# The order of five queues: all attention products ahead of the first FFN group's matmuls

## What is computed

```python
csum = jnp.cumsum(jax.nn.log_sigmoid(ftilde), axis=-1)       # ftilde, itilde: linear gates of [q,k,v]
Dtilde = where(tril, csum_i - csum_j, -inf) + itilde_j
max_d = jnp.max(Dtilde, axis=-1, keepdims=True)
Ctilde = jnp.einsum('bhid,bhjd->bhij', qh, kh) * jnp.exp(Dtilde - max_d) / TAU
maxit = jnp.maximum(jnp.abs(jnp.sum(Ctilde, -1, keepdims=True)), jnp.exp(-max_d))
Htilde = jnp.einsum('bhij,bhjd->bhid', Ctilde, vh) / (maxit + 1e-06)
x = x + groupnorm_per_head(Htilde) * gn_w + gn_b
xf = layernorm(x)
h = jax.nn.silu(jnp.einsum('nd,edf->nef', xf, w1))
routed = jnp.einsum('ne,ned->nd', combine, jnp.einsum('nef,efd->ned', h, w2))
shared = jax.nn.sigmoid(xf @ shared_gate_w) * ((jax.nn.silu(gate) * up) @ shared_down)
out = x + routed + shared
```

## Time and profile before

| | |
|---|---|
| median of 3 runs | 161.49 us (159.48 to 164.11) |
| the profiled execution's own time | 158.38 us |
| its span in the profile | 156.3 us |
| TensorE matmul busy | 132.2 us, 85% |
| VectorE busy | 133.6 us, 85% |
| ScalarE busy | 78.8 us, 50% |
| GpSimd busy | 66.4 us, 43% |
| granted TensorE clock, mean | 0.967 |

### The profile page before, as it was taken

How to read it: one execution, slowest core, us unless ns; L and a number is a source line. 1 busy time by engine, 2 the same in 40 slices (tenths; PEclk the granted TensorE clock), 3 DMA queues, 4 the chain that set the end, 5 groups by cost and what they waited for, 6 DMA issues and landing times.

```text
span 156.3 us, 4033 instructions
## 1 busy us (share of the span) xinstructions
PE 132.2 (85%) x1347; PEld 94.2 (60%) x1347; DVE 133.6 (85%) x511; ACT 78.8 (50%) x159; POOL 66.4 (43%) x134
## 2 busy tenths in 40 slices
PE   0566286499998978999989999988999999999990
PEld 0446175055764846536754688755677878788870
DVE  5999996947789899799999799999997989959882
ACT  3179967383124234553475635595567858251210
POOL 8765860898767899491554331026020000000000
PEclk9999999999968998579999999999999999999999
DMA  5998221471120001100000000000200011002002
GB/s 152 292 274 215 52 42 37 114 213 20 20 52 13 6 8 40 29 6 0 0 4 0 6 0 0 4 0 0 73 0 2 0 34 38 2 0 67 4 0 67
DMA packets 13268, 7.38 MB, mean 47 GB/s; under 512 B 1680, under 2 KB 12960, under 8 KB 13248
## 3 DMA queue, kind: packets, MB, share of 16 engines
q1 hardware_dynamic: 13072, 6.96, 17.7%
q10 hardware_dynamic: 176, 0.17, 0.5%
HBM read 4.83 MB, written 1.05 MB: 38 GB/s over the span
## 4 chain that ended last, share of the span: by engine, by line
PE 47%; DVE 35%; issue 7%; SPq 5%; DMA 1%; ACT 1%; POOL 1%; DVEq 1%; POOLq 0%
PE bank L984 16%; PE bank L966 12%; DVE xs L1441 7%; PE bank L888 5%; PE bank L929 5%; PE bank L900 4%; SPq L264 3%; PE bank L872 3%; DVE ct L1285 2%; DVE qblk L1447 2%; DVE st L1178 2%; DVE vsum L1213 2%; DVE newt L1356 1%; DVE vs L1343 1%; DMA mr<-pm 1%
## 5 line engine op out<-in xcount | busy, mean ns | idle before, releaser
L1441 DVE SCALAR_TENSOR_TENSOR xs<-bank,comb,xs 128x128 f32<-128x128 f32 x128 | 35.9, 344 | 4.9 <-PE bank L984 4.2
L984 PEld LDWEIGHTS bank<-w,hh 128*128 128x128 f32 x288 | 36.3, 191 | 5.6 <-issue 1.1
L984 PE MATMUL bank<-w,hh 128*128 128x128 f32 x288 | 37.9, 277 | 0.7 <-DVE xs L1441 0.3
L647 ACT ACTIVATE hh<-bank 128x512 f32<-128x512 f32 x36 | 21.3, 597 | 25.6 <-PE bank L966 25.2
L966 PE MATMUL bank<-xnT,w 128*128 128x512 f16 x120 | 31.1, 382 | 0.8 <-DVE hh L1430 0.8
L929 PEld LDWEIGHTS bank<-vx,ct 64*64 64x64 f32 x512 | 16.0, 135 | 3.9 <-issue 3.4
L966 PEld LDWEIGHTS bank<-xnT,w 128*128 128x128 f16 x120 | 11.4, 99 | 9.9 <-issue 2.7
L929 PE MATMUL bank<-vx,ct 64*64 64x17 f32 x512 | 17.2, 208 | 0.1
L403 POOL TENSOR_TENSOR kw<-vx,tok 128x128 f32<-128x128 f32 x32 | 12.9, 432 | 8.2 <-DVE tok L1275 4.2
L888 PE MATMUL bank<-qblk,kT 128*64 128x512 f16 x96 | 15.1, 420 | 1.2 <-DVE ct L1285 1.2
L600 ACT ACTIVATE dd<-bank 128x512 f32<-128x512 f32 x16 | 9.2, 592 | 13.1 <-PE bank L872 12.6
(11 more groups left out here) (129 smaller groups left out, 231.2 us busy)
## 6 DMA issues: line engine op xcount, KB each, us to landing
xs<-in_x SPq DMA_DIRECT2D x4, 256.0 KB, 4.8
cx<-in_ctx SPq DMA_DIRECT2D x4, 256.0 KB, 5.2
qblk<-qT SPq DMA_DIRECT2D x32, 32.0 KB, 2.0
w<-in_w SPq DMA_DIRECT2D x2, 512.0 KB, 4.4
out<-xs SPq DMA_DIRECT2D x4, 256.0 KB, 2.5
mr<-in_mr SPq DMA_DIRECT2D x2, 384.0 KB, 6.7
gl<-in_gl SPq DMA_DIRECT2D x1, 384.0 KB, 5.1
mr<-pm SPq DMA_DIRECT2D x12, 8.0 KB, 1.9
```

The lines of the kernel that those rows point to most:

```text
L647: A.activation(hh[:, e], pH[e % 2][:, :], ACT.Silu).then_inc(silu_ready, 1)
L984: ins = pe.matmul(pO[n % 2][:, t * P:(t + 1) * P], hh[:, e, t * P:(t + 1) * P], w2[:, e], start=True, stop=True)
L1441: ins = V.scalar_tensor_tensor(ob[:, a], pO[n % 2][:, t * P:(t + 1) * P], comb[:, f % 2, t, e:e + 1], (ob if e else x2)[:, a], ALU.mult, A ...
```

## The change

Only the order of calls in the lists of TensorE, VectorE, ScalarE and GpSimd changes. No instruction is added, except that ScalarE's list has four table loads fewer (six instead of ten); the list of transfers is untouched. On TensorE the five FFN calls named above go behind `intra(7, 1)`, and the order of `hidden` and `down` behind that point is another. On ScalarE all silus of group 0 stand behind `router_exp(1)`. On VectorE the accumulates of group 0 stand behind `token_stats(6)`, and `gate_up(f)` stands earlier. Some calls of the attention stage are swapped with a neighbour. The new order on TensorE (the old one is on the lines with a minus):

```diff
@@ tensor: swaps ahead of batch 4
             turn_q(1)
+            turn_ctx(3)
             turn_gates(0)
-            turn_ctx(3)
...
             intra(0, 1)
+            inter(1)
             pairs(2, 0)
-            inter(1)
...
             scores(2, 0)
+            pairs(2, 1)
             states(2)
-            pairs(2, 1)
@@ tensor: from batch 4 on
             scores(4, 0)
-            hidden(0, 0)
             inter(5)
-            hidden(0, 1)
             scores(4, 1)
             intra(4, 0)
             scores(5, 0)
             intra(4, 1)
             scores(5, 1)
-            down(0, 0)
+            intra(5, 0)
             states(6)
-            intra(5, 0)
             pairs(6, 0)
             intra(5, 1)
+            scores(6, 0)
             inter(6)
-            scores(6, 0)
             pairs(6, 1)
+            pairs(7, 0)
             xn_turn(1)
+            pairs(7, 1)
+            scores(6, 1)
             states(7)
-            pairs(7, 0)
-            pairs(7, 1)
-            hidden(0, 2)
-            scores(6, 1)
             intra(6, 0)
+            scores(7, 0)
             inter(7)
-            scores(7, 0)
             intra(6, 1)
             scores(7, 1)
+            intra(7, 0)
             logits(1)
+            intra(7, 1)
+            hidden(0, 0)
+            hidden(0, 1)
+            xn_turn(2)
+            hidden(0, 2)
+            hidden(0, 3)
+            down(0, 0)
+            hidden(0, 4)
+            hidden(0, 5)
             down(0, 1)
-            intra(7, 0)
-            intra(7, 1)
-            hidden(0, 3)
...
@@ scalar
             router_exp(0)
-            silu_table()
-            silu(0, 0)
-            silu(0, 1)
             normalise_again(2)
             square(4)
-            exp_table()
             head_log(4)
...
+            head_log(6)
+            head_exp(6)
+            square(7)
+            router_exp(1)
+            silu_table()
+            silu(0, 0)
+            silu(0, 1)
+            silu(0, 2)
...
@@ vector
             masked_states(6)
-            accumulate(0, 0)
             sums(5)
             refine_root(4)
+            weigh_scores(6, 0)
             between(6)
-            weigh_scores(6, 0)
...
+            between(7)
             weigh_scores(7, 1)
+            denominator(6)
             take_logits(1)
-            between(7)
+            variance(6)
+            sums(7)
+            route_top(1)
+            denominator(7)
+            route_chosen(1)
+            refine_root(6)
+            route_weights(1)
+            variance(7)
+            token_stats(6)
+            accumulate(0, 0)
             accumulate(0, 1)
...
@@ gpsimd
             residual(1)
-            token_shift(0)
             residual_bias(4)
             w1_low(1)
             w1_low(2)
             w1_low(3)
+            w1_low(4)
+            token_shift(0)
             token_root(1)
...
             residual_bias(6)
+            residual_bias(7)
             token_shift(2)
-            residual_bias(7)
```

More of the change, by code:

```diff
@@ L678, in _ @@
             decay(1, 0)
+            floor_factor(1)
             decay(1, 1)
-            floor_factor(1)
             w1_high()
+            square(0)
             decay(2, 0)
-            square(0)
             head_log(0)
@@ L691, in _ @@
             head_exp(1)
+            square(2)
             normalise_again(0)
-            square(2)
             normalise_again(1)
@@ L714, in _ @@
             head_exp(4)
+            square(5)
             normalise_again(3)
-            square(5)
             decay(6, 1)
+            decay(7, 0)
             xn_high(1)
-            decay(7, 0)
             decay(7, 1)
@@ L723, in _ @@
             normalise_again(4)
-            silu_table()
-            silu(0, 2)
             square(6)
             normalise_again(5)
+            head_log(6)
[6 more added lines that the diff above has]
+            silu(0, 2)
             silu(0, 3)
-            square(7)
             silu(0, 4)
             silu(0, 5)
+            normalise_again(6)
             silu(0, 6)
@@ L746, in _ @@
             silu(1, 3)
-            normalise_again(6)
             silu(1, 4)
@@ L752, in _ @@
             silu(1, 8)
-            normalise_again(7)
+            exp_table()
+            head_log(7)
+            router_exp(2)
+            head_exp(7)
+            silu_table()
             silu(2, 0)
-            xn_high(3)
             silu(2, 1)
-            exp_table()
-            router_exp(2)
-            silu_table()
             silu(2, 2)
             silu(2, 3)
+            normalise_again(7)
             silu(2, 4)
+            xn_high(3)
             silu(2, 5)
@@ L765, in _ @@
             silu(2, 7)
+            silu(2, 8)
             exp_table()
@@ L768, in _ @@
             silu_table()
-            silu(2, 8)
             silu(3, 0)
@@ L1098, in _ @@
             hidden(1, 3)
-            down(1, 0)
+            down(0, 4)
             hidden(1, 4)
             hidden(1, 5)
+            down(0, 5)
+            hidden(1, 6)
+            down(0, 6)
+            hidden(1, 7)
+            down(0, 7)
+            hidden(1, 8)
+            down(0, 8)
+            hidden(1, 9)
+            down(1, 0)
+            hidden(2, 0)
             down(1, 1)
-            hidden(1, 6)
-            hidden(1, 7)
+            hidden(2, 1)
             down(1, 2)
-            hidden(1, 8)
-            hidden(1, 9)
+            hidden(2, 2)
             down(1, 3)
-            hidden(2, 0)
+            hidden(2, 3)
+            hidden(2, 4)
+            down(1, 4)
+            down(1, 5)
             xn_turn(3)
-            down(1, 4)
-            hidden(2, 1)
+            hidden(2, 5)
+            down(1, 6)
             logits(3)
[L1114 to L1122, removed]
             hidden(2, 6)
             hidden(2, 7)
+            down(1, 7)
+            hidden(2, 8)
+            down(1, 8)
+            hidden(2, 9)
+            down(2, 0)
+            hidden(3, 0)
             down(2, 1)
+            hidden(3, 1)
             down(2, 2)
-            hidden(2, 8)
+            hidden(3, 2)
             down(2, 3)
             down(2, 4)
-            hidden(2, 9)
-            hidden(3, 0)
+            hidden(3, 3)
             down(2, 5)
             down(2, 6)
-            hidden(3, 1)
-            hidden(3, 2)
+            hidden(3, 4)
             down(2, 7)
-            hidden(3, 3)
-            hidden(3, 4)
             down(2, 8)
+            hidden(3, 5)
             down(3, 0)
-            hidden(3, 5)
             down(3, 1)
+            hidden(3, 6)
             down(3, 2)
-            hidden(3, 6)
             down(3, 3)
+            hidden(3, 7)
             down(3, 4)
-            hidden(3, 7)
             down(3, 5)
@@ L1460, in _ @@
             ctx_low(1)
+            ctx_low(2)
             gate_tokens(0)
-            ctx_low(2)
             value_means(1)
@@ L1482, in _ @@
             running_max(1)
+            max_of_decay(1)
             m_high(1)
-            max_of_decay(1)
             masked_states(0)
```

59 lines of the change are left out of this document (20 added, 39 removed).

## The result

The changed kernel is slower: 167.53 us median of 4 runs (166.35 to 168.86) against 160.49 us of before (158.83 to 164.11), ratio 1.050, 95% interval 1.034 to 1.066. The forecast was 163.1 us. The ratios leave out runs that lie over 1.5% above the fastest of their kernel, and some of those are runs whose clock fell further, so I give the median of all runs of a kernel beside its ratio.

The account below looks back on a forecast made before the run. No single limit: VectorE and TensorE share attention, then TensorE's remaining FFN matmuls plus gaps set the end. +3.7 - 2.1 + 1.9 - 1.9 + 0 = +1.6 us, carried over as 1.0% to 163.1 us; range 159.5 to 167.0.

Parts of the forecast that it names:

- FFN work taken out: Three hiddens and two downs leave the attention stage, so the part behind it must hold 3.7 us more.
- Attention's gain: Attention, with two accumulates fewer on VectorE, ends 2.1 us earlier, near 90.9 us; ends of the range 0 and -3.7.
- The joint: Between attention and FFN, TensorE waits 1.9 us for the first silu behind router_exp(1); bounds 1.2 and 3 us.
- The old gaps: TensorE's 1.9 us of waits behind attention, 102.6 to 109.0 us in the old order, vanish; other end 0.
- What stays: Small waits from 109.0 to 152.4 us, 1.9 us in the old order, stay alike: 0, from -0.7 to +0.7.
- my walk: The new lists followed from 66 us on, with trace durations and about 0.1 us per semaphore passing.
- The swaps ahead of batch 4: Exchanges of neighbouring steps early in the attention stage would cost nothing that could be found: 0.
- The sum: All terms together: +1.6 us, profiled execution from 158.38 to 160.0 us, 1.0% more.
- The clock: Rival, chance 0.25: granted clock falls once in the attention stage, costing up to 1.7 or 3.4 us: 164.8 to 166.5 us.
- All three signs of being wrong: Attention ending later than 93 us, clock 0.5 behind 70 us, or TensorE waiting for accumulates between 95 and 125 us.

Follow-up runs that it names:

- The second set: Six later runs of the unmodified changed kernel beside the kernel before: median 164.36 us against 160.02 us, ratio 1.018.
- e_late: The kernel before with only the changes from batch 4 on, none of the swaps ahead of it: 162.14 us, ratio 1.023.
- e_early: The kernel before with only the swaps ahead of batch 4: 159.31 us, ratio 0.998.
- a_again: The changed kernel run once more, unmodified, beside the kernel before: median 164.36 us, ratio 1.018.
- e_stand: The changed kernel with 17 extra 512-column products at the five places from which the FFN calls went: median 164.03 us.
- e_best: The kernel before with the swaps ahead of batch 4 and four extra 512-column products ahead of scores: median 157.74 us, ratio 0.992.
- e_small: The changed kernel with eight extra small f32 products at each of 28 places, ahead of scores and intra of batches 1 to 7: 172.35 us.
- e_small4: The changed kernel with four extra small f32 products at each of 28 places, ahead of scores and intra: 170.89 us, ratio 1.047.

## Why the prediction was wrong

The direction was right, the size was not: forecast +1.0% and 163.1 us, measured +5.0% and 167.53 us, outside the range (167.0 at most). The second set, +1.8% and 164.36 us, lies inside the range. So how far off the forecast is depends on the set; that the clock was priced too low shows in both.

- **FFN work taken out, +3.7.** Right; the same matmuls stand behind attention at the same price.
- **Attention's gain, -2.1.** Right where the clock went as in before: 93.05 to 91.00 in `e_late`.
- **The joint, +1.9.** Right in size, 1.93 us. But it is not a price that can be taken back singly: bridging it won nothing, and 0.8 us in the profile after two more moves.
- **The old gaps, -1.9.** Right: the stretch behind the joint has none like those of the earlier trace rows.
- **What stays, 0.** Wrong by 1.0 us, where I had 0.7 us as the most. In before, 59.33 us lie between the end of attention and that of TensorE, with 55.6 us of work: 3.7 us lost, as priced. In `e_late` it is 64.14 us with 59.3 us of work: 4.8 us lost, 1.9 at the joint and 2.9 in small waits instead of 1.9. The chain of waits of after shows where most of that 1.0 us sits:

```profile
128.28 1.29 PE bank L962 x6
129.58 0.13 issue
129.71 1.13 PE bank L980 x8
130.84 0.10 issue
130.94 1.13 PE bank L980 x8
```

Two downs in a row take 1.13 us each instead of 0.89, with 0.13 and 0.10 us ahead of them, 0.7 us in all. They wait for accumulates, of which VectorE works off 16 instructions without a break from 128.44 us on, right behind `route_weights(2)` and `token_stats(7)`. I had named a wait for accumulates between 95 and 125 us as what would show me wrong. In `e_late`, whose clock matches my walk, this pair stands at 121.9 us.
- **The swaps ahead of batch 4, 0.** Right within the interval: `e_early` 0.998 (0.981 to 1.014).
- **The sum.** 2.7 us by order alone, where I had 1.6.
- **The clock.** This is the step that failed. I had it as a rival with a chance of 0.25 and priced one fall, at most 6.9 us and 3.4 us of cost, and only behind 86 us. The five profiles of the new order without extra products have 10.2 to 30.7 us of half clock, and in each the first fall began ahead of 86 us. I had said that VectorE's pace hides a fall in attention: it doesn't when a fall lasts, since TensorE was busy for 19.8 of 22.6 us there even at full clock. And I took 48.0 to 61.5, where the clock had held with TensorE alone in attention, as evidence that it would hold; it was one execution. All three signs of being wrong came: attention ended at 98.86 us, the clock was at half behind 70 us, and TensorE waited for accumulates (at 121.9 us in `e_late`).
- **What the clock cost.** From `e_late` to after, with 20.5 us more of half clock, TensorE ends 7.8 us later. From `e_late` to `a_again`, with 6.8 us more, it ends 4.5 us later; half rate on 6.8 us can cost 3.4 us at most, so something else is in it, and `xn_turn(0)` is already 1.3 us late there. Of the 7.0 us between the medians of the first set, 2.7 us are the order by `e_late`. The early swaps cost nothing in `e_early`, so the rest, the larger part, goes to half clock. Of the 4.3 us of the second set the order has the larger part. The recorded mean clocks fit that: even with 17 us of half clock set aside for the first 38 us (see the last section) and 4 us for the time behind TensorE's last work, I estimate at least 18 us of half clock for each of the first four runs (a share of 0.119 to 0.145 of the clock missing in 164 to 167 us), and at most 4.1 us for the 160.80 us run of the second (0.013 missing in 158.8 us).

The Trainium skill (TensorE: Matmul & The Clock Gate, Part 1) has the throttled state as the default, which activity releases. I had weighed that with the trace's one counterexample. The 30.7 us of half clock in after agree with the rule better than with my reading; that TensorE was busy for 16.62 of 17.05 us in the longest stretch and stayed at half does not follow from it. The other rule that I set aside, that of the Trainium skill (ScalarE: Activation LUTs, What ACT_TABLE_LOAD costs) of 1.38 us of drain at a change of table, has no counterpart in these rows: the silu starts 0.01 us behind the load in `e_late`.

What stays open: why the clock falls more in the new order, and whether putting the dense products back would hold it (`e_stand` was inconclusive); why the first four runs of the changed kernel lay within 166.4 to 168.9 us and six later ones spread from 160.8 to 167.6; how much of it is TensorE's idle time and how much the kind of its products; and a version of the new order with attention's own work made denser, which wasn't tried.

## What to carry to other kernels

Here the order that separates a stage of small, waiting matmuls from a stage of dense ones came with more half clock (10.2 to 30.7 us against 0 to 10.2 us), and in the first set of runs that cost more than all the waits that I had counted. So I would price a clock that may fall by the share of the stage in which TensorE would become the bound at half rate, and not by the falls that one profile happens to show. I would compare kernels between executions with the same clock, as `e_late` with before. A wait that one sees at a joint may lie beside a second engine's lateness: bridging it paid here only after calls of the other engines were moved too, and then 0.8 of 1.9 us in one profile.

## What the runs showed of the hardware

- The same instructions ran with 17.05 us of half clock from 46.95 us on in one execution and with 3.40 us from 49.25 us on in another (30.7 and 17.1 us in all), and the time went from 168.86 to 165.59 us. The granted clock is part of this kernel's spread.
- The recorded clock can read full where it is not. In before it reads 1.00 from the start, but a set of four transposes takes 1.06 to 1.12 us up to 16 us and 0.66 us at 81; in after the recorded clock is 0.50 from 19.7 to 36.7 us. The point at which this first part ends differed too: scores take 0.84 us from about 36 us on in most profiles, and in `e_best` and `e_small` only behind 44 us. So the sums in the table leave out 6 to 7 us in these two, and the mean clock of a run, which depends on whether this part was recorded, gives bounds only.
- A stretch at half clock can be full of work: TensorE was busy for 16.95 of 17.10 us (`e_small4`, 73.5 to 90.6), and in before for 6.90 of 6.90 us.
